# A ring of 12 gathered tiles instead of 32, transposes a piece earlier, ten extra matmuls at the start, and two VectorE instructions exchanged

## The chip, the cores and the metric

The kernel runs on one core of a Trainium2 chip. The metric is the device time of one execution in microseconds (us); the median of several executions is quoted. The core's engines are TensorE (PE in the profile, its weight loads PEld), VectorE (DVE), ScalarE (ACT), GpSimd (POOL) and SyncE (SP), which here only starts DMAs.

## What is computed

A recommendation tower for 512 samples: 26 embedding tables are looked up, a dense vector of 128 values joins each sample, all pairwise dot products are formed, and three layers follow.

```python
e = jnp.stack([tbl_0[ids[:, 0]], ..., tbl_25[ids[:, 25]]], axis=1)       # (512, 26, 128)
sd = jnp.einsum('bfd,bd->bf', e, dense)
ss = jnp.einsum('bfd,bgd->bfg', e, e)
z = concatenate([dense, sd, ss[:, iu, ju]], axis=1)                     # iu < ju, 325 pairs
h = concatenate([z, dense], axis=1)                                     # (512, 607)
h = jnp.maximum(h @ W_top1 + b_top1, 0.0)                               # 512 wide
h = jnp.maximum(h @ W_top2 + b_top2, 0.0)                               # 256 wide
y = h @ W_top3                                                          # (512, 1)
```

## The kernel before, in words

All is kept in float32. The transposed embeddings of every sample stand in the tile `ET` (128 values on the partitions, 32 columns for each sample, 27 of them used). They come there in two ways.

**Look-ups by matmul.** Ten tables of 1000 rows (`ONE`) are loaded whole, in six groups (`SIDE`). ScalarE rounds a table to the fp32r format and VectorE forms the remainder (`part`, L558: the "two splits"). VectorE also builds one-hot matrices from the ids (`make_onehot`, L552), one for each of eight chunks `k` of 125 rows, into a ring of `RING` = 7 slots (L39); a one-hot waits until the chunk that used its slot is done (L550). TensorE multiplies split tables by one-hots (L342, two matmuls for each table and chunk), and ScalarE copies the result from PSUM to `ET` (L480, L482). On VectorE's queue a group is: the lower splits of its tables, then its eight one-hots.

**Gathers.** Sixteen larger tables (`MAIN`) are read by indirect DMAs that GpSimd issues (L294). The samples are split into 16 blocks of 32, `b0` to `b15`; a block needs four gathers of 128 rows. The gathered rows go to the tile `rows`, a ring of `ROWS_RING` = 8 * GB = 32 tiles (L46), eight blocks. Before the first gather of block n >= 8 GpSimd waits until TensorE has transposed block n - 8 (L292, L293, semaphore `staged`). TensorE transposes a block by four matmuls with the identity into a PSUM bank `stage` (L325), and ScalarE copies it to `ET` (L470). The transposes stand at places that are written out by hand: the table `AMID` (L200) puts b0 to b7 between chunks of the look-ups (b7 behind the last), `SOON` (L203) puts a block directly behind the gram matmuls of a piece, and `LATER` (L204) behind the layers of a piece.

**The pieces.** When the look-ups are done, TensorE goes through nine pieces of the batch (`PIECES`: seven of 64 samples, two of 32). `gram_piece` (L371) makes for each sample one 27x27 product of its `ET` columns with themselves; each is a weight load and a matmul, and in float32 each of these runs as two instructions, so that a piece of 64 is 128 weight loads and 128 matmuls. Piece p needs blocks 2p and 2p + 1. ScalarE (L492) and VectorE (L568) move the products to `Z`, VectorE folds the two triangles with masks (L579, L586), and TensorE runs the first layer (L387, L398) and the second (L413, L415) of the 128 samples before. VectorE ends with the third layer (L599). Piece p + 2 reuses the PSUM bank of piece p, so it waits for the moves of p. Nothing inside a piece waits for anything.

On each engine's queue the order is fixed. GpSimd's holds only the identity matrix (`ident`, used by the transposes) and the 64 gathers. SyncE's holds the loads. ScalarE's begins with three small loads, among them the bias `b1c`, read 4 bytes at a time.

Of the kernel before, what the change touches and what calls it, by code (L numbers as in the profile page):

```python
# [11 lines left out]
P = 128  # L12
# [7 lines left out]
HC = H1 // P  # L20
# [14 lines left out]
KR = 8  # L35
RAW = 3

SIDE = [[0], [1, 2], [3, 4], [5, 6], [7, 8], [9]]
RING = 7  # L39


BS = 32
NB = B // BS
GB = BS * NM // P
NG = NB * GB
ROWS_RING = 8 * GB  # L46

# [57 lines left out]
def dlrm_tower(nc, x, out):  # L107
    ctx = ExitStack()
    with ctx:
        def sb(name, shape, dt=F32):  # L110
            return ctx.enter_context(nc.sbuf_tensor(name, shape, dt))

        def pb(name, shape):
            return ctx.enter_context(nc.psum_tensor(name, shape, F32))
# [10 lines left out]
        denseT = sb("denseT", [P, B])  # L125
        rows = sb("rows", [P, ROWS_RING, D])
        raw = sb("raw", [P, RAW, KR * D])
        part = sb("part", [P, 4, 2, KR * D], FP32R)
        onehot = sb("onehot", [P, RING, 2 * B], FP32R)
        ident = sb("ident", [P, P])  # L130
# [5 lines left out]
        b1c = sb("b1c", [P, HC])  # L136
# [12 lines left out]
        second = [pb(f"second{i}", [P, 512]) for i in range(2)]  # L149
# [11 lines left out]
        w1d_in = sem("w1d_in")  # L161
# [7 lines left out]
        ident_ready = sem("ident_ready")  # L169
# [30 lines left out]
        AMID = {(0, 7): ["dense"], (1, 3): ["b0"], (2, 1): ["b1"], (2, 5): ["b2"], (3, 1): ["b3"],  # L200
                (3, 6): ["b4"], (4, 3): ["b5"], (4, 7): ["b6"], (5, 7): ["b7"]}

        SOON = {2: ["b8"], 3: ["b9"], 4: ["b10"]}  # L203
        LATER = {4: ["b11"], 5: ["b12", "b13"], 6: ["b14"], 7: ["b15"]}  # L204
        STAGED = [s for g, k in sorted(AMID) for s in AMID[g, k]] + [s for n in range(NP) for s in SOON.get(n, []) + LATER.get(n, [])]

        def bank_of(name):
# [79 lines left out]
        def _(pool):  # L287
            def gather(n, k):


                m = GB * n + k
                if m >= ROWS_RING and k == 0:  # L292
                    pool.wait_ge(*filled(f"b{n - ROWS_RING // GB}"))  # L293
                pool.indirect_dma_start(  # L294
                    out=rows[:, m % ROWS_RING, :], out_offset=None, in_=x["tables_gather"],
                    in_offset=bass.IndirectOffsetOnAxis(ap=idx[:, m:m + 1], axis=0),
# [12 lines left out]
        def _(pe):  # L309
            def transposes(name):  # L310
# [10 lines left out]
                else:  # L321
                    n = int(name[1:])
                    pe.wait_ge(gathered[n], 16 * GB)
                    for k in range(GB):
                        last = pe.transpose(bank[:, P * k:P * (k + 1)], rows[:, (GB * n + k) % ROWS_RING, :], ident[:, :])  # L325
                last.then_inc(staged, 1)

            def look_up(g):
# [4 lines left out]
                for k in range(KR):  # L333
                    pe.wait_ge(onehot_ready, KR * g + k + 1)
                    for j, i in enumerate(SIDE[g]):
# [5 lines left out]
                        for n in range(2):  # L341
                            last = pe.matmul(look_banks(g)[j], part[:, i % 4, n, D * k:D * (k + 1)],  # L342
                                             onehot[:, (KR * g + k) % RING, B * j:B * (j + 1)],
                                             start=(k == 0 and n == 0), stop=(k == KR - 1 and n == 1))
# [74 lines left out]
            def layers(p):  # L419
# [3 lines left out]
                for t, c in layer1_of(p):  # L423
                    layer1_dense(t, c)
                    layer1(t, c)

            for g in range(len(SIDE)):
                look_up(g)
            for p in range(NP):
                gram_piece(p)  # L430
                for name in SOON.get(p, ()):
                    transposes(name)
                layers(p)
                for name in LATER.get(p, ()):
                    transposes(name)
# [12 lines left out]
        @block.scalar  # L448
        def _(act):
            def upper_part(i):  # L450

                act.wait_ge(table_in[i], 16)
                if i >= 4:

                    act.wait_ge(chunk_done, KR * (group_of(i - 4) + 1))
                if i == 0:
                    act.copy(part[:, 0, 0, 2 * D:], raw[:, 0, 2 * D:]).then_inc(hi_ready, 1)
                else:
                    act.copy(part[:, i % 4, 0, :], raw[:, i % RAW, :]).then_inc(hi_ready, 1)  # L459

            def empty_stage(name):

                act.wait_ge(*filled(name))
                bank = bank_of(name)
                if name == "dense":
                    act.copy(denseT[:, :], bank[:, :])
                    act.copy(ETv[:, :, DENSE], bank[:, :]).then_inc(stage_taken, 1)
                else:
                    n = int(name[1:])
                    act.copy(ETv[:, BS * n:BS * (n + 1), 0:NM],  # L470
                             bank[:, :].rearrange("d (b v) -> d b v", v=NM)).then_inc(stage_taken, 1)

            def take_look_up(g):

                act.wait_ge(chunk_done, KR * (g + 1))
                for j, i in enumerate(SIDE[g]):
                    if i == NO - 1:

                        for at in (slice(0, P), slice(P, B)):
                            act.copy(ETv[:, at, V_ONE[i]], look_banks(g)[j][:, at]).then_inc(look_taken, 1)  # L480
                    else:
                        act.copy(ETv[:, :, V_ONE[i]], look_banks(g)[j]).then_inc(look_taken, 1)  # L482

            def move_gram(p):
                act.wait_ge(gram_done, p + 1)
                t = PIECES[p][0] // P
                if t >= ZT:

                    act.wait_ge(h1_done, HC * (t - ZT + 1))
                for i in (2, 3):  # L490
                    for dst, src in z_moves(p, (i,)):
                        last = act.copy(dst, src)  # L492
                    if i == 2:
                        for name in SOON.get(p, ()):
                            empty_stage(name)
                last.then_inc(gram_act, 1)

            def take_odd(t, c):

                act.wait_ge(h1_done, HC * t + c + 1)  # L500
                act.activation(h1T[:, t % 2, c, :], layer1_bank(t, c), ACT.Relu, bias=b1c[:, c:c + 1]).then_inc(h1_odd, 1)  # L501

            act.dma_start(rowid[:, :], x["rowid"]).then_inc(rowid_in, 16)
            act.dma_start(b2s[:, :], x["b_top2"].rearrange("(o n) -> o n", o=1)).then_inc(b2_in, 16)
            act.dma_start(b1c[:, :], x["b_top1"].rearrange("(c p) -> p c", p=P), allow_slow_non_contiguous=True).then_inc(w1d_in, 16)
            act.wait_ge(dve_consts, 1)
            act.activation(warm[:, :], zero[:, :], ACT.Identity, bias=zero[:, :])
            act.wait_ge(b2_in, 16)
            act.copy(b2h[:, 0, :], b2s[:, :]).then_inc(b2_high, 1)
            act.wait_ge(head_in, 16)  # L510
            act.copy(part[:, 0, 0, 0:2 * D], raw[:, 0, 0:2 * D]).then_inc(hi_ready, 1)
            for i in range(4):
                upper_part(i)
            for g in range(len(SIDE)):
                for k in range(KR):
                    if k == KR - 1:
                        take_look_up(g)
                    for name in AMID.get((g, k), ()):
                        empty_stage(name)
                for i in range(4, NO):  # L520
                    if group_of(i - 4) == g:
                        upper_part(i)
                if 1 <= g <= T:

                    t = g - 1
                    if t == 0:
                        act.wait_ge(look_taken, 3)
                        act.wait_ge(*emptied("dense"))
                    of = ETv[:, P * t:P * (t + 1), :]
                    act.copy(of[:, :, NV:NV + 3], of[:, :, LATE:NV])  # L530
                    act.copy(of[:, :, NV + 3:VP], of[:, :, LATE:LATE + VP - NV - 3]).then_inc(et_again, 1)
            act.wait_ge(w1d_in, 32)
            for p in range(NP):
                move_gram(p)
                if layer1_of(p):
                    take_odd(*layer1_of(p)[1])
                for name in LATER.get(p, ()):
                    empty_stage(name)
            for c in (1, 3):
                take_odd(T - 1, c)  # L540

        @block.vector
        def _(dve):
            def make_onehot(g, k):
                m = KR * g + k
                if k == 0:
                    dve.wait_ge(ids_in[g], 16)
                if m >= RING:

                    dve.wait_ge(chunk_done, m - RING + 1)  # L550
                w = B * len(SIDE[g])
                dve.tensor_scalar(onehot[:, m % RING, 0:w], ids16[:, B * SIDE[g][0]:B * SIDE[g][0] + w],  # L552
                                  rowid[:, k:k + 1], None, ALU.is_equal).then_inc(onehot_ready, 1)
# [59 lines left out]
                make_onehot(0, k)  # L613

            for g in range(1, len(SIDE)):
                for i in SIDE[g]:
                    lower_part(i, slice(0, KR * D)).then_inc(lo_ready, 1)
                for k in range(KR):
                    make_onehot(g, k)
            dve.wait_ge(b2_high, 1)  # L620
            dve.tensor_tensor(b2h[:, 1, :], b2s[:, :], b2h[:, 0, :].bitcast(F32), ALU.subtract).then_inc(b2_low, 1)
# [69 lines left out]
```

## Time and profile before

| | |
|---|---|
| median of 3 runs | 147.9 us (147.0 to 147.94) |
| the profiled execution | 147.75 us |
| its span, first to last instruction | 145.9 us |
| mean granted TensorE clock | 0.836 of 2.4 GHz |
| busy in the span: PE, PEld, DVE, ACT, POOL | 63%, 52%, 51%, 42%, 47% |
| bytes moved by DMA | 13.37 MB, of which 4.20 MB by the gathers |

The span is what the trace shows; about 1.9 us of the profiled execution lie around it. Times in the views are us from the start of the span. "issue" as what ended an idle stretch means that the engine waited for nothing that the profile shows.

### The profile page before, as it was taken

What the parts mean: (1) busy time and instruction counts of PE and PEld (TensorE: products, weight loads), DVE (VectorE), ACT (ScalarE), POOL (GpSimd) and SP (SyncE); (2) the same over time, 40 slices, a digit from 0 to 9 for tenths busy, and PEclk for the clock granted to TensorE, in tenths of its full rate; (3) what the DMA queues carried; (4) which work ended last, traced back from release to release, by engine and by line L of the source; (5) the groups of instructions that cost most, each with busy time, mean ns of one, the idle gap of its engine ahead of it and who ended that gap; (6) DMA issues with size and microseconds to landing.
All of it is one profiled execution on the core that took longest, in us unless ns stands there. A gap on an engine that the chain in (4) does not pass through costs nothing.

```text
span 145.9 us, 3331 instructions
## 1 busy us (share of the span) xinstructions
PE 91.8 (63%) x1420; PEld 75.7 (52%) x1420; DVE 74.3 (51%) x170; ACT 61.7 (42%) x131; POOL 68.5 (47%) x70
## 2 busy tenths in 40 slices
PE   0288999999699963221111001176879978988893
PEld 0256888888488841110100000175768868867791
DVE  1398999999958600000000000049986748576621
ACT  4423928668192850000000000049956768675511
POOL 3787887878787877777777775000000000000000
PEclk9999999999999997555555555555799999999999
DMA  3999949489941211122212212000000000000000
GB/s 61 264 393 364 275 109 313 130 163 380 362 126 44 54 48 46 54 54 54 54 54 54 54 54 53 1 7 4 4 0 4 4 4 0 4 4 0 4 2 1
DMA packets 6850, 13.37 MB, mean 92 GB/s; under 512 B 2354, under 2 KB 3507, under 8 KB 6835
## 3 DMA queue, kind: packets, MB, share of 16 engines
q1 hardware_dynamic: 4112, 8.95, 19.5%
q0 software_dynamic: 2048, 4.20, 10.3%
q8 instruction: 11, 0.18, 0.5%
q10 hardware_dynamic: 674, 0.01, 0.3%
q14 instruction: 5, 0.03, 0.1%
HBM read 13.15 MB, written 0.00 MB: 90 GB/s over the span
## 4 chain that ended last, share of the span: by engine, by line
PE 35%; issue 31%; POOL 15%; DMA 6%; ACT 6%; DVE 5%; DVEq 0%; ACTq 0%
POOL rows L294 15%; PE gram L371 10%; PE hidden L398 6%; DMA rows<-in_tables_gather,idx 5%; PE gram L342 5%; PE second L415 4%; ACT Z L492 4%; DVE Z L568 3%; PE hidden L342 3%; PE stage L325 3%; ACT ET L470 2%; PE hidden L387 1%; DMA idg<-in_ids_gather 1%; PE second L413 1%; PE stage L398 1%
## 5 line engine op out<-in xcount | busy, mean ns | idle before, releaser
L294 POOL DMA_INDIRECT rows<-in_tables_gather,idx x64 | 67.8, 1059 | 20.9 <-issue 19.2
L568 DVE COPY Z<-gram 32x112 f32<-32x112 f32 (+3 forms) x72 | 23.1, 321 | 54.0 <-PE gram L371 53.1
L492 ACT COPY Z<-gram 32x112 f32<-32x112 f32 (+1 forms) x72 | 23.2, 322 | 51.7 <-PE gram L371 50.9
L371 PE MATMUL gram<-ET 128*32 128x27 f32 x1024 | 18.5, 207 | 42.0 <-issue 37.6
L371 PEld LDWEIGHTS gram<-ET 128*32 128x32 f32 x1024 | 14.7, 124 | 46.4 <-issue 42.4
L552 DVE TENSOR_SCALAR onehot<-ids,rowid 128x1024 fp32r<-128x1024 int16 (+1 forms) x48 | 29.1, 662 | 3.6 <-DMA ids<-in_ids_one 2.0
L342 PE MATMUL gram<-onehot,part 128*128 128x512 f32 x80 | 22.3, 431 | 6.6 <-DVE part L558 6.2
L342 PEld LDWEIGHTS gram<-onehot,part 128*128 128x128 f32 x80 | 16.2, 209 | 10.6 <-DVE onehot L552 6.2
L342 PE MATMUL hidden<-onehot,part 128*128 128x512 f32 x80 | 19.8, 397 | 0.6 <-issue 0.6
L342 PEld LDWEIGHTS hidden<-onehot,part 128*128 128x128 f32 x80 | 14.6, 188 | 3.8 <-issue 0.8
L558 DVE TENSOR_TENSOR part<-raw,part 128x1024 fp32r<-128x1024 f32 (+2 forms) x11 | 12.1, 1123 | 2.9 <-ACT part L459 1.3
L398 PE MATMUL hidden<-Z,W1s 128*128 128x128 f32 x84 | 11.7, 278 | 1.1 <-DVE Z L579 1.1
L470 ACT COPY ET<-stage 128x512 f32<-128x512 f32 x16 | 9.4, 594 | 5.4 <-PE stage L325 4.9
L459 ACT CAST part<-raw 128x1024 fp32r<-128x1024 f32 x9 | 9.4, 1067 | 5.0 <-DMA raw<-in_tables_one 4.2
L398 PEld LDWEIGHTS hidden<-Z,W1s 128*128 128x128 f32 x84 | 10.5, 193 | 1.6 <-issue 0.8
L325 PE MATMUL stage<-ident,rows 128*128 128x128 f32 x64 | 10.1, 284 | 1.4 <-DMA rows<-in_tables_gather,idx 1.4
L415 PE MATMUL second<-W2s,h1T 128*128 128x256 f32 x32 | 9.3, 402 | 0.0
L325 PEld LDWEIGHTS stage<-ident,rows 128*128 128x128 f32 x64 | 7.8, 145 | 2.9 <-issue 1.8
L482 ACT COPY ET<-gram 128x512 f32<-128x512 f32 x5 | 5.3, 1152 | 4.2 <-PE gram L342 4.2
L415 PEld LDWEIGHTS second<-W2s,h1T 128*128 128x128 f32 x32 | 5.3, 189 | 1.3 <-ACT h1T L501 0.4
L482 ACT COPY ET<-hidden 128x512 f32<-128x512 f32 x4 | 4.2, 1164 | 3.4 <-PE hidden L342 3.4
L387 PE MATMUL hidden<-denseT,W1e 128*128 128x128 f32 x28 | 5.5, 285 | 0.0
(38 smaller groups left out, 39.5 us busy)
## 6 DMA issues: line engine op xcount, KB each, us to landing
raw<-in_tables_one SPq DMA_DIRECT2D x9, 512.0 KB
ids<-in_ids_one SPq DMA_DIRECT2D x4, 256.0 KB, 5.2
rows<-in_tables_gather,idx POOLq DMA_INDIRECT x64
W1s<-in_W_pairs SPq DMA_DIRECT2D x1, 768.0 KB
W1d<-in_W_dense SPq DMA_DIRECT2D x1, 512.0 KB
W2s<-in_W_top SPq DMA_DIRECT2D x1, 512.0 KB
raw<-in_tables_one SPq DMA_DIRECT2D x1, 384.0 KB
ids<-in_ids_one SPq DMA_DIRECT2D x2, 128.0 KB
```

What stands on the lines that cost most here:

```text
L294: pool.indirect_dma_start(out=rows[:, m % ROWS_RING, :], out_offset=None, in_=x["tables_gather"], in_offset=bass.IndirectOffsetOnAxis(ap=i ...
L325: last = pe.transpose(bank[:, P * k:P * (k + 1)], rows[:, (GB * n + k) % ROWS_RING, :], ident[:, :])
L342: last = pe.matmul(look_banks(g)[j], part[:, i % 4, n, D * k:D * (k + 1)], onehot[:, (KR * g + k) % RING, B * j:B * (j + 1)], start=(k == ...
L371: last = pe.matmul(gram[p % 2][32 * i:32 * i + 32, NV * j:NV * (j + 1)], ET[:, VP * b:VP * (b + 1)], ETv[:, b, 0:NV], start=True, stop=True)
L398: last = pe.matmul(layer1_bank(t, c), W1s[:, s, P * c:P * (c + 1)], Z[:, t % ZT, s, :], start=False, stop=(s == 0))
L415: last = pe.matmul(at, h1T[:, t % 2, c, :], W2s[:, c, :], start=False, stop=(c == HC - 1))
L470: act.copy(ETv[:, BS * n:BS * (n + 1), 0:NM], bank[:, :].rearrange("d (b v) -> d b v", v=NM)).then_inc(stage_taken, 1)
L482: act.copy(ETv[:, :, V_ONE[i]], look_banks(g)[j]).then_inc(look_taken, 1)
L492: last = act.copy(dst, src)
L552: dve.tensor_scalar(onehot[:, m % RING, 0:w], ids16[:, B * SIDE[g][0]:B * SIDE[g][0] + w], rowid[:, k:k + 1], None, ALU.is_equal).then_inc ...
L558: return dve.tensor_tensor(part[:, i % 4, 1, cols], raw[:, i % RAW, cols], part[:, i % 4, 0, cols].bitcast(F32), ALU.subtract)
L568: last = dve.tensor_copy(dst, src)
```

## The change

1. `ROWS_RING` goes from 8 * GB to 3 * GB: twelve tiles, three blocks. The wait of L293 becomes: before the first gather of block n >= 3, wait until block n - 3 is transposed.
2. `SOON` and `LATER`: b8 to b12 are transposed behind the gram matmuls of pieces 1 to 5 (before: b8, b9, b10 behind the gram matmuls of pieces 2, 3, 4; b11 behind the layers of piece 4; b12 behind the layers of piece 5). b13, b14, b15 stay.
3. TensorE first waits for the identity and multiplies it by itself ten times, into a PSUM bank that is overwritten later.
4. `RING`, the one-hots, from 7 to 8 slots.
5. In a group of two tables VectorE makes the first one-hot between the two lower splits.
6. The bias `b1c` is laid out on the host in the order in which it is used, and loaded as it lies.

```diff
-RING = 7
+RING = 8
+WARM = 10
@@
-ROWS_RING = 8 * GB
+ROWS_RING = 3 * GB
@@
-        SOON = {2: ["b8"], 3: ["b9"], 4: ["b10"]}
-        LATER = {4: ["b11"], 5: ["b12", "b13"], 6: ["b14"], 7: ["b15"]}
+        SOON = {1: ["b8"], 2: ["b9"], 3: ["b10"], 4: ["b11"], 5: ["b12"]}
+        LATER = {5: ["b13"], 6: ["b14"], 7: ["b15"]}
@@ the tensor engine's program
+            pe.wait_ge(ident_ready, 1)
+            for n in range(WARM):
+
+                pe.matmul(second[0][:, 0:P], ident[:, :], ident[:, :], start=True, stop=True)
             for g in range(len(SIDE)):
                 look_up(g)
@@ the scalar engine's program
-            act.dma_start(b1c[:, :], x["b_top1"].rearrange("(c p) -> p c", p=P), allow_slow_non_contiguous=True).then_inc(w1d_in, 16)
+            act.dma_start(b1c[:, :], x["b_top1"]).then_inc(w1d_in, 16)
@@ the vector engine's program
             for g in range(1, len(SIDE)):
-                for i in SIDE[g]:
+                for n, i in enumerate(SIDE[g]):
                     lower_part(i, slice(0, KR * D)).then_inc(lo_ready, 1)
-                for k in range(KR):
+                    if n == 0:
+
+                        make_onehot(g, 0)
+                for k in range(1, KR):
                     make_onehot(g, k)
@@ on the host
-        "b_top1": np.ascontiguousarray(inputs["b_top1"]), "W_top2": ...
+        "b_top1": np.ascontiguousarray(np.asarray(inputs["b_top1"]).reshape(HC, P).T), "W_top2": ...
```

## Rows read from the trace of the kernel before

**Rows 1.** Busy time by stretch: us, busy and count, clock, DMA share, GB/s
```profile
core 0: us, PE busy (x) PEld busy (x) DVE busy (x) ACT busy (x) POOL busy (x), PEclk, DMA share, GB/s
52.60:65.50 12.90, 3.51 (x58) 2.09 (x58) 0.00 (x0) 1.06 (x2) 9.55 (x12) 0.64 0.20 52
65.50:91.60 26.10, 2.70 (x13) 1.54 (x13) 0.00 (x0) 0.00 (x0) 18.83 (x20) 0.50 0.20 53
91.60:95.80 4.20, 0.61 (x3) 0.51 (x4) 0.00 (x0) 0.00 (x0) 0.00 (x0) 0.50 0.00 0
```

**Rows 2.** Who waited for whom: total us, times, longest
```profile
PE gram L371 <- issue: 37.6, 31, 2.6
DVE Z L568 <- PE gram L371: 53.1, 7, 46.2
```

**Rows 3.** Timeline of PE's matmuls around the gram pieces 0 and 1
```profile
52.66 0.45 PE L371 MATMUL gram<-ET 128*32 128x27 f32 x31
53.47 0.28 PE L371 MATMUL gram<-ET 128*32 128x27 f32 x5 [0.36 <-issue]
...
64.89 0.30 PE L371 MATMUL gram<-ET 128*32 128x27 f32 x2 [1.20 <-issue]
67.01 0.20 PE L371 MATMUL gram<-ET 128*32 128x27 f32 x1 [1.82 <-issue]
...
88.12 0.20 PE L371 MATMUL gram<-ET 128*32 128x27 f32 x1 [2.60 <-issue]
...
94.42 0.20 PE L371 MATMUL gram<-ET 128*32 128x27 f32 x1 [1.19 <-issue]
95.82 2.69 PE L371 MATMUL gram<-ET 128*32 128x27 f32 x182 [0.50 <-issue]
```

**Rows 4.** Timeline of POOL: gathers number 13, 44, 45 and 64
```profile
19.91 1.96 POOL L294 DMA_INDIRECT rows<-in_tables_gather,idx  x1 [0.30 <-issue]
...
64.22 0.94 POOL L294 DMA_INDIRECT rows<-in_tables_gather,idx  x1 [0.30 <-issue]
65.47 0.94 POOL L294 DMA_INDIRECT rows<-in_tables_gather,idx  x1 [0.30 <-issue]
...
89.17 0.94 POOL L294 DMA_INDIRECT rows<-in_tables_gather,idx  x1 [0.30 <-issue]
```

**Rows 5.** Timeline of PE: transposes of b0, b4, b7, b8, b15
```profile
17.98 0.60 PE L325 MATMUL stage<-ident,rows 128*128 128x128 f32 x4
...
38.74 0.63 PE L325 MATMUL stage<-ident,rows 128*128 128x128 f32 x4 [1.44 <-DMA rows<-in_tables_gather,idx]
...
51.98 0.60 PE L325 MATMUL stage<-ident,rows 128*128 128x128 f32 x4
...
101.83 1.12 PE L325 MATMUL stage<-ident,rows 128*128 128x128 f32 x4
...
133.46 0.60 PE L325 MATMUL stage<-ident,rows 128*128 128x128 f32 x4
```

**Rows 6.** Timeline of PE: gram matmuls of pieces 2 and 6
```profile
99.97 1.93 PE L371 MATMUL gram<-ET 128*32 128x27 f32 x128 [1.46 <-ACT Z L492]
...
124.35 1.29 PE L371 MATMUL gram<-ET 128*32 128x27 f32 x128 [0.73 <-ACT ET L470]
```

**Rows 7.** DMA queues of the page, the code's: packets, MB, share of 16 engines
```profile
q8 instruction: 11, 0.18, 0.5%
```

**Rows 8.** Timeline of PE: first look-ups
```profile
6.22 2.05 PE L342 MATMUL gram<-onehot,part 128*128 128x512 f32 x4 [6.22 <-DVE part L558]
...
14.20 3.94 PE L342 MATMUL hidden<-onehot,part 128*128 128x512 f32 x16 [0.61 <-issue]
```

**Rows 9.** Timeline of DVE: splits of tables 1 and 2, then one-hots
```profile
10.48 1.21 DVE L558 TENSOR_TENSOR part<-raw,part 128x1024 fp32r<-128x1024 f32 x1
12.25 1.23 DVE L558 TENSOR_TENSOR part<-raw,part 128x1024 fp32r<-128x1024 f32 x1 [0.56 <-issue]
13.40 5.39 DVE L552 TENSOR_SCALAR onehot<-ids,rowid 128x1024 fp32r<-128x1024 int16 x8
```

More of the change, by code:

```diff
@@ L680 @@
         "W_pairs": W_pairs.reshape(P, FOLD * H1), "W_dense": W_dense,
-        "b_top1": np.ascontiguousarray(inputs["b_top1"]), "W_top2": np.ascontiguousarray(inputs["W_top2"]),
+        "b_top1": np.ascontiguousarray(np.asarray(inputs["b_top1"]).reshape(HC, P).T), "W_top2": np.ascontiguousarray(inputs["W_top2"]),
         "b_top2": np.ascontiguousarray(inputs["b_top2"]), "W_top3": np.ascontiguousarray(inputs["W_top3"]),
```

## The prediction

> **What bounds the kernel now.** I read the table of busy time by stretch first, then the waits, then TensorE's timeline where the table looked wrong, then GpSimd's beside it.
>
> The kernel has three parts. Up to 52.6 us TensorE looks up; from 95.8 us on it works through the pieces to the end at 145.9 us. Between the two lies a hole: in 52.6 to 91.6 us, 39.0 us, it runs 71 matmuls, while VectorE is idle and GpSimd gathers evenly [rows 1]. The waits show the hole as 53.1 us in which VectorE waited for gram matmuls, 46.2 us of it once, and as 37.6 us in which TensorE itself waited for "issue", that is for nothing that the profile shows [rows 2]. The timeline shows its form. Piece 0 begins at 52.66 us, when b7 has been transposed; 31 matmuls run within half a microsecond, and then they come in ones and twos, 1.4 to 2.1 us apart around 65 us and 2.8 us apart around 88 us, until at 95.82 us the next 182 run in 2.69 us [rows 3]. No semaphore stands inside a piece, and the blocks b0 to b3, all that pieces 0 and 1 read, are there since long before.
>
> What ends the hole? The last of the 64 gathers is issued at 89.17 us and takes 0.94 us [rows 4], and from 91.6 us on the DMA share is 0.00 [rows 1]. Only then do the matmuls come closer: 1.4 us, 0.7 us, free [rows 3]. From the last packet to free issue are 95.82 - 91.6 = 4.2 us. After the hole the same instructions run 128 in 1.29 us [rows 6]. So the reading that I argue from is: while the gathers run, TensorE can't be fed short matmuls quickly; 31 are in its queue when a wait ends, the rest trickles. The look-ups, whose matmuls last 0.25 us each (16 in 3.94 us) [rows 8], ran beside the same gathers undisturbed. The trace shows that the two end together, not that one causes the other.
>
> **The change, part by part.**
>
> *The ring of 12.* It removes nothing; it adds waits on GpSimd. Block n may be gathered when block n - 3 is transposed. Behind a waiting gather nothing stands but later gathers, for which TensorE's transposes wait. b3 starts at 19.91 us and needs b0, done at 17.98 + 0.60 = 18.6 us: free. The gathers 13 to 44 have a pitch of (64.22 - 19.91)/31 = 1.43 us, so b7 (number 29) starts near 42.8 us and needs b4, done at 39.4 us: free. b10 ends with gather 44 at 65.2 us and needs b7, done at 52.6 us: free [rows 4, 5]. b11, in the kernel before at 65.47 us, needs b8, and b8 is now transposed behind piece 1. That is inside the hole. So GpSimd stops at 65.2 us with 44 of 64 gathers done, and cannot go on until TensorE has finished pieces 0 and 1. That is the whole change as I see it: the hole is cut short at about 65 us, and five blocks of gathers are put behind TensorE's progress.
>
> First release. The last packet lies 91.6 - 90.1 = 1.5 us behind the last gather's end, so at 66.7 us. The recovery then cost 4.2 us from a spacing of 2.8 us; at 65 us the spacing is that which the recovery had at its last two steps, 94.42 to 95.82 us [rows 3], so I take 1.4 us, bounds 0 and 4.2. TensorE is free at 68.1 us, finishes pieces 0 and 1 in 2.7 us (the row of 182), and transposes b8 in 1.1 us (the row at 101.83 us, with the clock low) [rows 3, 5]: b8 is done at 71.9 us.
>
> A round. From there each of b11 to b15 costs 4 gathers at (89.17 - 65.47)/19 = 1.25 us, 5.0 us in all [rows 4]. The next piece stands at most 6.1 - 1.3 = 4.8 us behind the transposes (the distance of two pieces less the 1.29 us of one [rows 6]), so it meets the gathers. If the trickle sets in again, the round is 5.0 + 1.5 to the last packet, a recovery, the 97 matmuls that were not queued at 2.69/182 each, 1.4 us, and the transposes, 0.6 us with the clock high and 1.1 us low, 0.9 us taken. For the recovery after a burst of only 5 us I take half of the first one, 0.7 us, again between 0 and 4.2. That makes 9.5 us. Moves and layers lie beside it: in the kernel before the pieces 2 to 6 begin (124.35 - 99.97)/4 = 6.1 us apart with all of them in between [rows 6], less than a round. b9 to b12 are done at 81.4, 90.9, 100.4 and 109.9 us. Piece 6 is released at 109.9 + 5.0 + 1.5 + 0.7 = 117.1 us and ends at 118.5 us. Before it ended at 124.35 + 1.29 = 125.6 us [rows 6], and from there the order is the old one, with all blocks landed. The gain is 7.1 us.
>
> *The transposes a piece ahead.* Four times four matmuls move in front of the layers, b8 also into the 1.46 us that TensorE waited in front of piece 2 [rows 6]. ScalarE's copy of b11 is then hidden by the layers, and a wait for it like the 0.73 us in front of piece 6 goes in front of piece 5; in front of piece 6 it stays, b13 being the last. Up to 1.8 us if the rounds don't swallow it, nothing if they do. Taken: nothing; kept for the rival without renewed trickle.
>
> *Ten identity matmuls.* The trace has no 128x128 matmul of the identity with the clock low but the transposes: 4 in 1.12 us [rows 5]. Ten are twenty instructions, so 2.2 us (at 0.11 us, 4 in 0.60 us less the latency) to 5.6 us, from about 1.5 us. The first look-up begins at 6.22 us [rows 8]: hidden, or 0.9 us late. Whatever TensorE gains there in clock, the second group begins when VectorE delivers: its first one-hot starts at 13.40 us behind both splits, the look-up at 14.20 us [rows 8, 9].
>
> *The exchange on VectorE, and one-hot slot 8.* The one-hot now comes behind the first split, 1.2 us (one split) earlier, but the second table's matmuls wait for the second split; up to 0.9 us. In front of b4's transposes TensorE waited 1.44 us for the landing of its rows, near 38.7 us [rows 5], and GpSimd, which sets that, moves by none of this. What is won ahead is lost there. Taken: nothing, bounds -0.9 and +0.9 us. If that cover is gone, 0.9 us ahead of piece 0 still changes nothing at 65.2 us, where GpSimd stops.
>
> *The bias.* One load of 2 KB on another layout, needed only behind the look-ups: nothing.
>
> The sum, against the profiled execution: 147.75 - 7.1 = 140.7 us; its 147.75 us is 0.15 us under the median, so 141 us against 147.9 us.
>
> **Where a page bears on it.** The hole could also be TensorE's code arriving late. The queues show 11 packets with 0.18 MB on the code queue in the whole span, 0.5% of the engines' time [rows 7], so little is moved, but it must be moved in time. The Trainium skill, "Runtime: NRT & Kernel Launch", section "Instruction fetch mechanics", says that an engine's instructions come in blocks of 256 that its sequencer fetches ahead, and that the cost of a block's border is mostly hidden. By that rule the hole isn't code, and the sum stands; by the opposite the third rival holds.
>
> **The rivals.**
>
> *No renewed trickle.* The hole may need a long run of gathers ahead of it, as there was in the kernel before (from 19.91 us and earlier without a pause [rows 4]). For it: the spacing grew slowly, from 1.4 to 2.8 us over 20 us [rows 3]. Against: the trickle set in within half a microsecond of the first short matmuls. Then b8 is done at 71.9 us, the gathers of b11 to b15 follow in 25 us, to 97 us, and the pieces from 2 on take what they took before, 145.9 - 99.97 = 45.9 us, from 72.5 us on, less up to 1.8 us: span 117 to 118.4 us, time 119.5 us.
>
> *The recovery is long each time* (the slow side). If it costs 4.2 us whenever gathers stop, b8 is done at 74.7 us, a round is 13.0 us, b12 is done at 126.7 us, piece 6 ends at 126.7 + 10.7 + 1.4 = 138.8 us, 13.2 us later than before: 161 us. The point from which it decides: with rounds of 9.5 + x us the gain of 7.1 us is used up at 5x = 7.1, so at a recovery of 0.7 + 1.4 = 2.1 us. What speaks for it is the one recovery that was measured; against, that it came from a deeper state.
>
> *The stop of the gathers is no release.* If the hole has another cause (code, or its own length), TensorE is free near 95.8 us as before, b8 is done at 99.6 us, and 25 us of gathers plus 1.5 us end at 126 us, ahead of b15's transposes at 133.46 us [rows 5]. Then only 0 to 1.8 us are won: 146 to 148 us. This is also the case that the change doesn't do what it does here.
>
> *No hole at all*, should another start shift it away. b15 lands at 91.6 us as before and what lies behind its transposes, 145.9 - 133.46 = 12.4 us [rows 5], follows: about 106 us. Nothing speaks for it but that the cause isn't shown.
>
> **How the numbers follow.** Renewed trickle with a short recovery 0.40; none 0.24; long recovery 0.18; no release 0.13; no hole 0.05. The likeliest gives 141 us, its own range with recoveries between 0 and 2.1 us being 136 to 148 us. The range over all keeps out the case without a hole and the upper part of the slow one: 117 to 155 us. A difference of about 1% is what a measurement of this kernel can tell. Faster by more: 0.37 of the first, 0.24, 0.03 of the no-release case and 0.05, together 0.69; slower by more: 0.18 and 0.02, that is 0.20; the rest, 0.11, within it.
>
> **What the profile after would show.** POOL idle in front of b11's first gather, from 65 us until TensorE's transposes of b8. TensorE's "issue" idle ending within 2 us after the last packet, near 68 us. Then for each of pieces 2 to 6 either a gap of 5 to 8 us behind 31 matmuls (renewed trickle) or 128 matmuls in under 2 us (none). The first sum falls if gather 44 doesn't end near 65 us, if TensorE is still starved with GpSimd idle, or if the look-ups end far from 52.6 us. Recoveries after pauses are the number that decides the sign.

## The result

The changed kernel takes 134.7 us (median of 4 runs, 134.48 to 135.56) where the kernel before takes 147.9 us (147.0 to 147.94). The ratio is 0.914, 95% interval 0.910 to 0.919. The forecast was 141 us with a range of 117 to 155 us. The profiled execution took 134.65 us, its span 132.8 us: 13.1 us less than the span before.

Four lines of the changed kernel's table of busy time by stretch answer to [rows 1]: until the gathers stop, until TensorE is free, until the last gather, the rest (columns: stretch and length, busy us and instructions of PE, PEld, DVE, ACT, POOL, granted clock, DMA share, GB/s).

```profile
52.60:66.70 14.10, 4.12 (x73) 2.57 (x74) 0.00 (x0) 1.12 (x2) 10.72 (x12) 0.58 0.20 52
66.70:69.20 2.50, 0.41 (x3) 0.13 (x1) 0.00 (x0) 0.00 (x0) 0.00 (x0) 0.50 0.11 26
69.20:110.50 41.30, 30.59 (x801) 27.14 (x801) 21.69 (x66) 21.27 (x58) 18.90 (x20) 0.76 0.12 33
110.50:132.80 22.30, 17.51 (x352) 15.02 (x352) 10.73 (x40) 9.61 (x31) 0.02 (x1) 1.00 0.02 6
```

The hole that lasted from 52.6 to 95.8 us ends at 69.2 us. The waits of the changed kernel, against [rows 2] (engine, line, waited for: us in total, times, longest):

```profile
DVE Z L573 <- PE gram L372: 38.4, 8, 20.7
PE gram L372 <- issue: 22.6, 27, 1.9
POOL rows L295 <- PE stage L326: 20.3, 5, 7.9
```

TensorE's waiting for "issue" fell from 37.6 to 22.6 us, and there is a wait that did not exist: GpSimd stands 20.3 us in front of five blocks of gathers. GpSimd's timeline shows the first two of these waits and the last gather (start, us, line, count, idle before and its releaser), against [rows 4]:

```profile
65.73 0.95 POOL L295 DMA_INDIRECT rows<-in_tables_gather,idx  x1 [0.30 <-issue]
74.53 0.95 POOL L295 DMA_INDIRECT rows<-in_tables_gather,idx  x1 [7.85 <-PE stage L326]
...
82.63 0.95 POOL L295 DMA_INDIRECT rows<-in_tables_gather,idx  x1 [3.41 <-PE stage L326]
...
109.57 0.95 POOL L295 DMA_INDIRECT rows<-in_tables_gather,idx  x1 [0.30 <-issue]
```

TensorE's timeline has the other side of it, against [rows 3, 5, 6]:

```profile
53.30 0.63 PE L326 MATMUL stage<-ident,rows 128*128 128x128 f32 x4 [1.22 <-DMA rows<-in_tables_gather,idx]
53.86 0.61 PE L372 MATMUL gram<-ET 128*32 128x27 f32 x42
...
69.26 2.70 PE L372 MATMUL gram<-ET 128*32 128x27 f32 x184 [0.50 <-issue]
73.48 0.19 PE L372 MATMUL gram<-ET 128*32 128x27 f32 x1 [1.51 <-issue]
73.61 0.65 PE L326 MATMUL stage<-ident,rows 128*128 128x128 f32 x4
74.19 0.60 PE L372 MATMUL gram<-ET 128*32 128x27 f32 x46
...
80.24 1.08 PE L372 MATMUL gram<-ET 128*32 128x27 f32 x61 [1.10 <-issue]
81.25 1.12 PE L326 MATMUL stage<-ident,rows 128*128 128x128 f32 x4
...
96.17 1.29 PE L372 MATMUL gram<-ET 128*32 128x27 f32 x128
97.39 0.66 PE L326 MATMUL stage<-ident,rows 128*128 128x128 f32 x4
...
110.74 0.47 PE L372 MATMUL gram<-ET 128*32 128x27 f32 x33 [1.49 <-issue]
111.55 1.02 PE L372 MATMUL gram<-ET 128*32 128x27 f32 x95 [0.33 <-issue]
```

The reader is to see the turns. The gathers stop at 66.7 us, TensorE is free at 69.26 us, b8 is transposed at 74.3 us, the gathers start again, and piece 2 gets 46 matmuls through and trickles until 80.24 us, one microsecond behind the fourth gather. Piece 4 (96.17 us) has its 128 matmuls in one row: its gathers had ended at 95.2 us.

Where the 13.1 us come from: piece 2 begins at 74.19 instead of 99.97 us, 25.8 us earlier. From there to the start of piece 6 the kernel before needed 24.4 us, the changed one 110.74 - 74.19 = 36.6 us: 12.2 us are given back in the turns. Piece 6 itself takes 1.8 instead of 1.3 us. Behind it the two kernels are alike.

### The profile page after: what moved, and what is told of

Its sections match the earlier page's. It is cut to its first block, busy times and chain, and to the rows that moved or that the text cites. A ratio compares the mean times of both kernels' runs of the same rounds, so it can differ in the third digit from the quotient of the medians.

```text
span 132.8 us, 3371 instructions
## 1 busy us (share of the span) xinstructions
PE 99.1 (75%) x1440; PEld 82.4 (62%) x1440; DVE 73.8 (56%) x170; ACT 62.0 (47%) x131; POOL 70.1 (53%) x70
## 3 DMA queue, kind: packets, MB, share of 16 engines
q0 software_dynamic: 2048, 4.20, 11.1%
## 4 chain that ended last, share of the span: by engine, by line
PE 36%; POOL 29%; issue 25%; ACT 3%; DMA 3%; DVE 2%; DVEq 0%
POOL rows L295 29%; PE gram L372 13%; PE hidden L399 8%; PE second L416 5%; PE stage L326 4%; PE hidden L388 2%; ACT Z L497 2%; DMA rows<-in_tables_gather,idx 2%; PE second L414 2%; DVE Z L573 1%; DMA idg<-in_ids_gather 1%; PE stage L399 1%; ACT ET L475 1%; DVE h2w L604 0%; ACT h1T L506 0%
## 5 line engine op out<-in xcount | busy, mean ns | idle before, releaser
L295 POOL DMA_INDIRECT rows<-in_tables_gather,idx x64 | 69.4, 1085 | 39.6 <-PE stage L326 20.3
L372 PE MATMUL gram<-ET 128*32 128x27 f32 x1024 | 18.2, 206 | 24.0 <-issue 22.6
L343 PE MATMUL gram<-onehot,part 128*128 128x512 f32 x80 | 20.5, 405 | 0.5 <-DVE onehot L557 0.5
L343 PEld LDWEIGHTS gram<-onehot,part 128*128 128x128 f32 x80 | 15.1, 195 | 4.0 <-DVE onehot L557 1.0
L399 PE MATMUL hidden<-Z,W1s 128*128 128x128 f32 x84 | 14.1, 315 | 0.6 <-DVE Z L584 0.6
L326 PE MATMUL stage<-ident,rows 128*128 128x128 f32 x64 | 10.8, 296 | 3.5 <-DMA rows<-in_tables_gather,idx 3.5
L399 PEld LDWEIGHTS hidden<-Z,W1s 128*128 128x128 f32 x84 | 13.0, 231 | 0.8 <-DVE Z L584 0.8
L416 PE MATMUL second<-W2s,h1T 128*128 128x256 f32 x32 | 10.2, 436 | 0.0
L416 PEld LDWEIGHTS second<-W2s,h1T 128*128 128x128 f32 x32 | 5.8, 206 | 1.6 <-ACT h1T L506 0.4
L506 ACT ACTIVATE h1T<-hidden,b1c 128x128 f32<-128x128 f32 x7 | 2.6, 367 | 8.3 <-PE hidden L399 8.3
L388 PE MATMUL hidden<-denseT,W1e 128*128 128x128 f32 x28 | 6.2, 316 | 0.0
```

Source lines behind the costliest of these rows:

```text
L295: pool.indirect_dma_start(out=rows[:, m % ROWS_RING, :], out_offset=None, in_=x["tables_gather"], in_offset=bass.IndirectOffsetOnAxis(ap=i ...
L372: last = pe.matmul(gram[p % 2][32 * i:32 * i + 32, NV * j:NV * (j + 1)], ET[:, VP * b:VP * (b + 1)], ETv[:, b, 0:NV], start=True, stop=True)
L399: last = pe.matmul(layer1_bank(t, c), W1s[:, s, P * c:P * (c + 1)], Z[:, t % ZT, s, :], start=False, stop=(s == 0))
L416: last = pe.matmul(at, h1T[:, t % 2, c, :], W2s[:, c, :], start=False, stop=(c == HC - 1))
```

## The experiments

The theory from the prediction: GpSimd's gathers starve TensorE's short matmuls, and a pause of the gathers frees it. The rival: the hole is of another kind (TensorE's code, or something that the ten matmuls or the rebuild move). Times stand beside those of the kernel before on the same chip and the same occasion. No chip of these experiments was used on more than one occasion.

**The ring alone, and all but the ring.**

```diff
 ring_alone: the kernel before with
-ROWS_RING = 8 * GB
+ROWS_RING = 3 * GB
 all_but_ring: the changed kernel with
-ROWS_RING = 3 * GB
-RING = 8
+ROWS_RING = 8 * GB
+RING = 7
```

> The kernel before with the ring of 12 tiles and nothing else of the change. Theory 1 (GpSimd's gathers starve TensorE's short matmuls, so a pause of the gathers frees it): the gathers stop behind number 44 near 65 us, TensorE is free near 69 us as in the changed kernel, the time is within 2 us of the changed kernel's 134.7 us, a little above because b8 is transposed only behind piece 2. Theory 2 (the hole comes from another part, such as the code's place moved by the ten matmuls): the hole lasts to 95 us as before, 146 to 148 us.

> The changed kernel with the ring of gathers back at 32 tiles (and 7 one-hot slots, for room). Theory 1: the hole is back, from about 53.5 us to 4 us behind the last gather, 95 us; time 145 to 147.5 us, the difference to 147.9 us being what the earlier transposes are worth. Theory 2: the hole stays short, 133 to 136 us.

**Gathers left out, and gathers replaced by plain loads.**

```diff
 no_late_gathers: the kernel before with
-            for n in range(NB):
+            for n in range(8):
 and no wait for the gathers of b8 to b15
 plain_loads: the same, and on GpSimd's and on SyncE's queue
+            for m in range(8 * GB, NG):
+                for i in range(3):
+                    ...
+                    pool.memset(pad[:, :], 0.0).then_inc(paced, 1)
+            for m in range(8 * GB, NG):
+                sp.wait_ge(paced, 3 * (m - 8 * GB + 1))
+                ...
+                sp.dma_start(rows[:, m % ROWS_RING, :], x["tables_gather"][P * m:P * (m + 1), :]).then_inc(gathered[m // GB], 16)
```

> The kernel before without the gathers of blocks b8 to b15 (half of the gathered rows are left out; the transposes read what the ring holds from b0 to b7). GpSimd is idle from about 50 us on. Theory 1: no hole; pieces 0 and 1 take about 3 us from 52.7 us on and the kernel ends 43 us earlier, 103 to 106 us. Theory 2 (code supply or a length of its own): the hole of 40 us stays, about 147 us.

> The kernel before with the gathers of b8 to b15 replaced by plain loads of the same size and number (rows 128m to 128m+127 of the tables instead of the gathered ones), issued by SyncE, each behind three memsets of GpSimd that keep about the gathers' pace. The same bytes arrive, but GpSimd issues no indirect DMA. If GpSimd's issuing of gathers starves TensorE: no hole, about 105 us. If the traffic of small transfers into SBUF does it: a hole of the length of the loads, 120 us or more.

These four ran on one chip, and on it the kernel before took 108.8 us (19 runs, 107.25 to 110.94), not 147.9 us. The ring alone took 109.4 us (ratio 1.003, 0.998 to 1.009), all but the ring 110.2 us (1.006, 1.001 to 1.011), no late gathers 107.5 us, plain loads 108.1 us (one execution each of these two). None has a hole, though in the first two GpSimd gathers without a pause. The numbers of both theories for the first two runs were missed, because all of them took a hole in the kernel before for granted; and the last two say nothing here, since there was no hole to remove. Two lines of the busy times of all_but_ring there:

```profile
52.60:65.50 12.90, 8.54 (x399) 7.50 (x399) 8.34 (x25) 8.57 (x23) 9.85 (x11) 0.80 0.21 57
65.50:91.60 26.10, 24.28 (x693) 21.41 (x692) 17.12 (x53) 17.19 (x47) 19.05 (x21) 0.97 0.22 56
```

The gathers are those of [rows 1]: 11 and 21 in the two stretches (12 and 20 there), at 56 to 57 GB/s. But TensorE runs 399 and 693 matmuls beside them where the kernel before had 58 and 13. So "short matmuls beside gathers" is not enough for a hole; something outside the kernel is needed too. It went with the chip as far as was seen, but each chip was seen on one occasion only, so that something of the occasion is not excluded. "A chip with the hole" below stands for such a chip on its occasion.

The gathers are not free where there is no hole either: the 128 matmuls of piece 6 took 1.82 us beside them (all_but_ring, at 85.12 us) and 1.29 us without them (no_late_gathers, at 83.19 us), both with the granted clock at 1.00.

**Both kernels again.** No edit.

> The changed kernel once more, beside the kernel before. In the four runs just made the kernel before took 108.8 us, not 147.9 us, and none had the hole. Theory 1 (the hole comes with the chip or with something outside the kernel, and the change pays only where it is there): both near 109 us where the kernel before has no hole, ratio 0.99 to 1.01; where it has, 147 and 135 us. Theory 2 (a property of the kernel's own placement that a rebuild can undo): the changed kernel keeps its own holes, about 122 us beside 109 us.

> The kernel before, for its trace. Where there is no hole: pieces 0 and 1 run at full speed behind b7's transposes while the gathers go on, the last transposes (b15) stand near 95 us, close behind the last gather, and the span is about 107 us; TensorE's code queue shows its packets near the pieces' borders. Where there is one: 147 us with the trickle from 52.7 to 95.8 us.

On another chip the kernel before took 146.7 us (7 runs) and the changed one 133.5 us, ratio 0.906 (0.896 to 0.916), and one more execution of the kernel before 147.5 us, with the trickle up to 95.3 us. The gain repeats where the hole is. Between the two theories this does not decide, because they differ only where the kernel before has no hole, and there the changed kernel was never run. In all, the kernel before ran on six occasions: 147.9, 146.7, 147.0 and 147.2 us with it, 108.8 and 108.7 us without.

**The same questions on chips with the hole.**

> The kernel before without the gathers of b8 to b15 (half of the gathered rows are left out) once more, for a chip on which the kernel before has the hole (if it has none here, this says nothing new, 107 us). Theory 1 (there the gathers starve TensorE's short matmuls): no hole, 105 to 108 us beside 147 us. Theory 2 (on such a chip TensorE's code is slow to come, whatever GpSimd does): a hole in pieces 0 and 1, 120 us or more.

> The kernel before with plain loads from SyncE in the place of the gathers of b8 to b15, once more, for a chip with the hole (107 to 109 us where there is none). If GpSimd's issuing of indirect DMAs starves TensorE: 106 to 109 us. If transfers in small packets into SBUF while TensorE starts short matmuls do it: a hole as long as the loads, 130 to 148 us.

> The kernel before with the ring of 12 tiles alone, once more, for a chip with the hole (109 us where there is none). Theory 1: the gathers stop near 65 us, TensorE is free near 69 us; b8 is transposed behind piece 2 instead of piece 1, so the gathers go on some 4 us later than in the changed kernel, and the later transposes come behind the layers: 134 to 140 us. If the ring were not the part that matters: 147 us.

Beside 147.0 us the kernel without late gathers took 107.4 us and the one with plain loads 105.9 us: no hole in either. The busy times from 52.6 to 65.5 us, first without the gathers, then with plain loads:

```profile
52.60:65.50 12.90, 8.76 (x438) 8.30 (x439) 9.99 (x30) 9.99 (x28) 0.00 (x0) 0.74 0.02 6
```

```profile
52.60:65.50 12.90, 9.03 (x461) 8.58 (x451) 10.37 (x31) 9.77 (x28) 10.07 (x50) 0.74 0.31 86
```

With plain loads the DMA share is 0.31 and 86 GB/s arrive, more than the 52 GB/s of the gathers [rows 1], GpSimd is busy 10 of 12.9 us, and TensorE runs 461 matmuls. So on such a chip the gathers as GpSimd issues them make the hole; neither bytes into SBUF nor a GpSimd that is busy with memsets do. Each of the two kernels ran once, but 40 us are far outside the spread of a few us between executions. The plain loads are not the gathers in every other way, though: their 2.10 MB came in 4608 packets and on the queue of SyncE's loads, all the gathers' 4.20 MB in 2048 packets on GpSimd's own queue. Which of these it is (the issue, the queue, the packets) is not shown.

The ring alone took 139.9 us, ratio 0.954 (0.949 to 0.959). Expected were 134 to 140 us. The gathers end at 65.0 us there and TensorE is free at 67.3 us: the small ring by itself cuts the hole short. It wins 7 us of the 13, and its GpSimd shows where the other part lies:

```profile
89.54 0.94 POOL L294 DMA_INDIRECT rows<-in_tables_gather,idx  x1 [2.85 <-PE stage L325]
...
98.29 0.94 POOL L294 DMA_INDIRECT rows<-in_tables_gather,idx  x1 [0.30 <-issue]
108.59 0.94 POOL L294 DMA_INDIRECT rows<-in_tables_gather,idx  x1 [9.36 <-PE stage L325]
```

b10 and b11 are transposed close to each other there, ahead of and behind the layers of piece 4. So two blocks (b13, b14) are gathered in one go, 89.5 to 99.2 us; piece 5, begun at 93.1 us, trickles until 100.9 us; and GpSimd, done, waits 9.36 us for b12's transposes behind the layers. With the earlier transposes each piece releases one block, and the turns are even. That the other 6 us come from this is read from the traces: no run had the ring and the earlier transposes without the ten matmuls, the exchange, the bias and the eighth slot.

**All but the ring on a chip with the hole, and a tighter pairing.**

```diff
 late_b15: the changed kernel with
-                    pool.wait_ge(*filled(f"b{n - ROWS_RING // GB}"))
+                    pool.wait_ge(*filled(f"b{n - (3 if n < 10 else 2)}"))
+                if n == NB - 1 and k == 0:
+                    pool.wait_ge(gram_done, 7)
```

> The changed kernel with the ring of gathers back at 32 tiles (and 7 one-hot slots) once more, for a chip with the hole (109 to 110 us where there is none). The ring alone gave 139.9 us beside 147.0 us, the whole change 133.5 us beside 146.7 us, so the rest is worth 5 to 6 us with the ring. Theory 1a (what the rest gives is the earlier transposes, which let the gathers and the pieces take turns; without the small ring there are no turns): the hole is back, 145 to 148 us. Theory 1b (the rest has a worth of its own): 141 to 142 us.

> The changed kernel with the waits of the gathers drawn tighter: from b10 on block n waits for block n - 2 instead of n - 3, and b15 waits besides for the end of piece 6. On a chip with the hole, theory 1 (each piece runs only while the gathers rest, and TensorE is free about 1 us behind the last gather): the first stop comes a block earlier, at 61 us, the last gather ends about 112 us as before, but piece 6 has run by then: 1.5 to 3 us less than the changed kernel, ratio to the kernel before 0.885 to 0.90. A rival (every round costs the same 7.8 us, and there is now one more): 3 to 5 us more than the changed kernel, ratio 0.93 to 0.94. Without the hole 0.99 to 1.02.

All but the ring took 147.1 us beside 147.2 us (10 and 13 runs; ratio 0.997, 0.993 to 1.002). The earlier transposes, the ten matmuls, the exchange and the bias are worth nothing without the small ring, as 1a had it; the eighth one-hot slot was left out of this run as well. The run also corrected the theory. Its hole begins before any short matmul, in the last look-ups; TensorE's timeline:

```profile
50.29 0.73 PE L343 MATMUL hidden<-onehot,part 128*128 128x512 f32 x2 [1.03 <-issue]
52.64 1.22 PE L343 MATMUL hidden<-onehot,part 128*128 128x512 f32 x2 [1.62 <-issue]
55.92 1.22 PE L343 MATMUL hidden<-onehot,part 128*128 128x512 f32 x2 [2.06 <-issue]
62.22 1.22 PE L343 MATMUL hidden<-onehot,part 128*128 128x512 f32 x2 [5.08 <-issue]
77.62 1.22 PE L343 MATMUL hidden<-onehot,part 128*128 128x512 f32 x2 [14.18 <-issue]
```

and the other engines of that run: ScalarE's copy behind finished look-ups, two of VectorE's last one-hots, and GpSimd's first gather of b15 ("remote" stands where the profile names no engine as what ended the wait):

```profile
61.68 1.93 ACT L487 COPY ET<-gram 128x512 f32<-128x512 f32 x2 [13.49 <-remote]
...
61.68 0.48 DVE L557 TENSOR_SCALAR onehot<-ids,rowid 128x512 fp32r<-128x512 int16 x1 [5.82 <-remote]
77.08 0.49 DVE L557 TENSOR_SCALAR onehot<-ids,rowid 128x512 fp32r<-128x512 int16 x1 [14.92 <-remote]
...
83.36 0.94 POOL L295 DMA_INDIRECT rows<-in_tables_gather,idx  x1 [0.30 <-issue]
90.11 0.94 POOL L295 DMA_INDIRECT rows<-in_tables_gather,idx  x1 [5.81 <-remote]
```

TensorE's five gaps are put down to "issue", but each ends 0.05 us behind the end of a one-hot (77.08 + 0.49 = 77.57, 77.62 us): TensorE waits for VectorE here. VectorE stood 14.9 us and ScalarE 13.5 us in front of single instructions whose inputs were ready; the look-ups that ScalarE copies had ended at 47.4 us, and the slots of the one-hots were free at 48.5 us at the latest. GpSimd itself was held too. b15's first gather needs b7's transposes, which ended at 79.7 us, and the gather before it was over at 84.3 us; but it began at 90.11 us, within half a microsecond of ScalarE's next copy (89.81 us) and of piece 0 (90.29 us), about 4.9 us behind the last packet. So what is held up beside the gathers on these chips is neither TensorE alone nor short matmuls alone: instructions came late on all four engines, on GpSimd where it waited for another. VectorE stood 4.5, 1.6, 2.8, 5.8 and 14.9 us in front of its last five one-hots. Behind the last four gathers the pieces run free from 95.7 us there too. Of the kernel before, the second trace shows it as well, ahead of any short matmul:

```profile
58.17 1.05 ACT L480 COPY ET<-hidden 128x128 f32<-128x128 f32 x2 [6.98 <-remote]
```

The look-ups that this copy takes had ended at 51.9 us, and piece 0 began behind it, at 58.65 us. That the other traces show the trouble first inside piece 0, where nothing is waited for, may be because TensorE needs 256 instructions in little more than a microsecond there; that is argued, not shown.

late_b15 took 133.5 us beside 147.2 us, ratio 0.900 (0.891 to 0.909). The changed kernel had 0.906 (0.896 to 0.916) and 0.914 (0.910 to 0.919) on other chips. The first overlaps with it, the second lies just above it, and the two kernels were never timed on one chip, so a gain over the changed kernel is not shown. Piece 6 ran in one row as expected (106.4 us), and the stop came a block earlier, with turns of 7.4 to 7.9 us; but the first gather of b15 starts at

```profile
108.48 0.94 POOL L297 DMA_INDIRECT rows<-in_tables_gather,idx  x1 [4.74 <-PE gram L374]
```

and three more follow, to 113.2 us, so that piece 7 trickles (112.0 to 114.5 us) in the place of piece 6. The slow-side rival, one more round at full price and a ratio of 0.93 to 0.94, fell.

**Keeping TensorE's queue full.**

```diff
 filler4: the kernel before, in gram_piece
+                        if p < 4 and i == 3:
+                            pe.matmul(second[0][:, :], part[:, 0, 0, 0:P], onehot[:, 0, 0:B], start=True, stop=True)
```

> The kernel before with one long matmul (128x128 weights, 512 columns, about 0.2 us, its result never read) behind every fourth sample of pieces 0 to 3, so that TensorE's queue does not run dry while the gathers go on. Left to itself this costs 64 x 0.2 us, 13 us less what the moves of the products hide. Theory 3a (the trickle sets in only when the short matmuls empty the queue): on a chip with the hole it is gone, 110 to 122 us beside 147 us. Theory 3b (beside a gather the supply of instructions is slow whatever the queue holds; look-ups get by because each lasts 0.2 us): the hole stays until 4 us behind the last gather, and with it the pieces 0 and 1 as before, 147 to 155 us. Without the hole: 110 to 118 us.

133.8 us (2 runs) beside 108.7 us: the chip had no hole, so the question stays open, and the 110 to 118 us expected for that case were missed. What it shows is the price: a group of eight short matmuls and a long one takes 0.63 us (starts at 52.26, 52.88, 53.51 us), three times the 0.2 us that I had put down, 64 times in the pieces.

## Why the prediction was right, and where it was off

The direction, the range and the likeliest case (renewed trickle, short recovery) came out; the size was 7.1 us against 13.1. Part of it is luck: the forecast rests on a hole in the kernel before, and on two of six occasions there was none.

*The stop.* Right: GpSimd stopped behind b10, at 66.7 instead of 65.2 us. I had called b7 free; it was free of the ring, but its rows landed 1.2 us behind TensorE's need, and piece 0 began at 53.86 us.

*The release.* Right in kind and size: from the last gather's end to free issue 69.26 - 66.68 = 2.6 us, against 2.9. That a stop of the gathers is the release, and not a coincidence as the trace before could not exclude, is shown by the ring alone (0.954, hole ended at 67.3 us) and by the kernel without late gathers (107.4 beside 147.0 us).

*The way to b8's transposes.* Forecast 71.9 us, measured 74.3 us: 1.2 us from the two points above and 1.51 us that I did not have, less 0.3 us because the transposes were shorter. TensorE waits for "issue" in front of the last matmul of piece 1, at 73.48 us, with no gather going on. The rows fit a border of its code, which no run tested by itself: between 70.5 and 73.4 us the code queue moves one packet of 16 KB and no gather runs, and on the chip without a hole all_but_ring shows such pauses too. From the first to the second TensorE runs 128 matmuls and their 128 weight loads, and the second stands inside piece 1, where nothing is waited for:

```profile
52.61 1.81 PE L372 MATMUL gram<-ET 128*32 128x27 f32 x127
55.69 1.81 PE L372 MATMUL gram<-ET 128*32 128x27 f32 x128 [1.27 <-issue]
59.41 0.18 PE L372 MATMUL gram<-ET 128*32 128x27 f32 x1 [1.91 <-issue]
```

The Trainium skill, "Runtime: NRT & Kernel Launch", section "Instruction fetch mechanics", has blocks of 256 instructions and calls the cost of their borders mostly hidden. The blocks agree with these rows; the cost does not in the first pieces, where 256 instructions last under 2 us: 1.3 and 1.9 us stay visible, and 1.0 us once more in piece 2 (63.17 us). From piece 3 on each piece has its 128 matmuls in one row and no pause shows.

*A round.* This is the term that was mis-sized: 9.5 us forecast, (105.55 - 74.26)/4 = 7.8 us measured from b8's transposes to b12's. The gathers took the 5.0 us. From the last gather's end to free issue it was 80.24 - 79.23 = 1.0 us, where I had 1.5 + 0.7 = 2.2. The burst's last packets arrive until about 80.2 us, so the way to the last packet was 1.0 us and the recovery behind it nothing. The trickle was also milder: 61 to 87 matmuls were left, 0.9 to 1.1 us, and not 97. Over four rounds this is 38.0 - 31.3 = 6.7 us; with piece 6, which ended 7.0 us behind b12's transposes and not 8.6, it is 8.3 us. Less the 2.4 us by which b8 was late, 5.9 us are left, and that is the difference between 13.1 and 7.1 within 0.1 us.

The sign that I had named for the pieces came out in part. TensorE stood 5.5 us in front of the rest of piece 2, inside my 5 to 8 us, but 1.9 us in piece 3 and 2.6 us in piece 5, and piece 4 had no gap. The layers, with the granted clock at 0.51, lay beside the burst and took the place of the trickle (90.20 to 96.17 us ahead of piece 4), so that round took its 7.8 us without any trickle.

*The transposes a piece ahead.* I took nothing, and at most 1.8 us. Without the ring all the other parts together are worth nothing (0.997), but with it about 6 us: 0.954 for the ring alone, 0.906 and 0.914 for the whole change, each beside the kernel before on its own chip. The traces put these 6 us down to the earlier transposes. I had costed them as ScalarE's copy in front of a piece and missed that under the new rule each transpose is what lets a block of gathers go. The rounds of my sum were those of the changed order, so the sum did hold this gain; the part had no price of its own.

*The start.* Right: the ten matmuls ran from 1.52 to 6.2 us; TensorE reached b4's transposes earlier and waited there 2.28 instead of 1.44 us [rows 5].

*The rivals.* "No renewed trickle" fell on pieces 2, 3 and 5. "Long recovery" fell: 2.6 us once, about 1 us each time after. "The stop is no release" fell. "No hole at all" is what two of the six occasions showed in the kernel before: about 109 us against my 106. I had it as an effect of the change, at 0.05. It comes from outside the kernel, and there the ring alone moves nothing. The whole changed kernel was not run on such a chip; its two halves are 1.003 and 1.006 there.

## What to carry to other kernels

Where an engine waits for "issue" as long as another engine goes on issuing DMAs, treat it as a stall like any other, cut the DMAs into bursts, and give each burst a place beside work that can bear it; here one third of the stall's 39 us was won that way: half of it by a ring that is made smaller, the rest only together with the other changes. Before tuning against such a stall, time the kernel on several chips and occasions: the same program ran in 109 and in 147 us, and a change that wins 9% on the one kind won nothing on the other as far as its parts were tried. Where a small ring couples two queues, the order of the consumer's work is part of the ring: place each release so that one piece frees one block.

## What the runs showed of the hardware that I had not expected

- The same kernel took 147 us on four occasions and 109 us on two, on five different chips at least. On the first kind, while GpSimd issues indirect DMAs at a 1.25 us pitch, instructions come late on every engine, GpSimd included where it waits for another (up to 14.9 us, all but the ring); on the second kind, with the same gathers at the same pace, there is no such stall, only 128 short matmuls in 1.82 instead of 1.29 us. What does it, in the chip or outside, stays open. So does why the gathers of the first 43 us do no harm; the plain loads of the tables run beside them until about 40 us, but that is a coincidence in time and was not tried.
- As many plain loads from SyncE as there were late gathers, with a GpSimd that was busy with memsets, did no harm on a chip of the first kind (105.9 us, one execution).
- After a burst of four gathers TensorE is free 1.0 us behind the last one's end, with the last packet. After gathers without a long pause up to 66.7 us it was 2.6 us, up to 84.3 us (all but the ring) 5.5 us to the first instruction of any engine, and up to 90.1 us 95.82 - 90.11 = 5.7 us [rows 1, 3, 4].
- A long full-width matmul behind every eight short matmuls on 32 columns makes the group 0.63 us long, at a granted clock of 1.00. The long one alone takes 0.25 us in the look-ups [rows 8] and eight short ones 0.08 us (1.29 us for 128) [rows 6].
